# Raw self-attention scores copied to SBUF and masked there, in a two-layer transformer kernel on one Trainium2 core

## What is computed

```python
# layer 0
Q, K, V = relu(x @ Wq.T + bq), relu(ctx @ Wk.T + bk), relu(ctx @ Wv.T + bv)
scores = einsum('bqd,bkd->bqk', Q_, K_) / sqrt(d)
scores = where(key_mask == 0, NEG, scores); scores = where(tril == 0, NEG, scores)
attn = softmax(scores) * query_mask
x = gamma * norm(attn @ V_ + x) + beta
# layer 1
q, k, v = heads(split(layernorm(x) @ sa_wqkv))
wei = softmax(where(padding, -inf, where(causal, q @ k.T * scale, -inf)))
result = x + merge(wei @ v) @ sa_wproj + sa_bproj
q2 = heads(layernorm(result) @ ed_wq); k2, v2 = heads(split(layernorm(ctx) @ ed_wkv))
result = result + merge(softmax(q2 @ k2.T * scale) @ v2) @ ed_wproj + ed_bproj
result = result + relu(layernorm(x) @ ff_w1 + ff_b1) @ ff_w2 + ff_b2
```

## Time and profile before

| | us |
|---|---|
| median of three runs | 370.42 |
| the profiled execution, its own time | 373.18 |
| its span in the profile | 371.3 |
| TensorE busy with matmuls | 353.6 (95%) |
| VectorE busy | 224.9 (61%) |
| ScalarE busy | 172.1 (46%) |
| GpSimd busy | 52.6 (14%) |

### The profile page before, as it was taken

The page is one execution under the profiler, slowest core; times in us unless marked ns, Lnnn a source line. Parts: engine busy times, 40 slices in busy tenths (PEclk is TensorE's granted clock), DMA queues, the critical chain, the costliest instruction groups (busy, mean ns, idle before and its releaser), DMA issues.

```text
span 371.3 us, 9714 instructions
## 1 busy us (share of the span) xinstructions
PE 353.6 (95%) x4154; PEld 267.0 (72%) x4154; DVE 224.9 (61%) x563; ACT 172.1 (46%) x301; POOL 52.6 (14%) x67
## 2 busy tenths in 40 slices
PE   8997899999999999999999998999999999999995
PEld 4575778987886857875678676765986758785673
DVE  3289998915658677646686646478954374354511
ACT  2336755273682341565515155593353455505142
POOL 2003351122240100012210012132110121000000
PEclk9789999999999999999999999999999999999999
DMA  6757012100000012000000001000000000000000
GB/s 188 209 215 302 26 26 72 39 2 2 2 25 2 3 26 85 2 14 0 17 1 3 2 15 71 2 14 14 3 0 4 2 2 12 3 2 14 2 2 25
DMA packets 5044, 13.43 MB, mean 36 GB/s; under 512 B 669, under 2 KB 2837, under 8 KB 4746
## 3 DMA queue, kind: packets, MB, share of 16 engines
q1 hardware_dynamic: 4712, 12.72, 10.4%
q10 hardware_dynamic: 290, 0.10, 0.1%
HBM read 11.89 MB, written 0.92 MB: 35 GB/s over the span
## 4 chain that ended last, share of the span: by engine, by line
PE 81%; DVE 11%; ACT 5%; issue 2%; POOL 0%; DVEq 0%
PE ring L503 39%; PE ring L757 8%; PE acc L661 7%; PE ring L636 5%; PE ring L771 5%; PE ring L616 4%; DVE negmax L1053 4%; ACT exps L877 3%; PE ring L610 3%; PE ring L648 2%; PE ring L680 2%; DVE negmax L1032 1%; PE ring L815 1%; PE ring L628 1%; PE ring L722 1%
## 5 line engine op out<-in xcount | busy, mean ns | idle before, releaser
L1053 DVE TENSOR_REDUCE negmax<-ring 112x2 f32<-112x750 f32 x64 | 56.9, 935 | 32.9 <-PE ring L757 32.8
L877 ACT ACTIVATE exps<-ring 125x896 f32<-125x896 f32 x48 | 41.4, 915 | 56.7 <-PE ring L771 56.6
L1264 POOL TENSOR_SCALAR_AFFINE_SELECT exps<-exps 112x896 f32<-112x896 f32 x32 | 31.3, 1000 | 111.5 <-ACT exps L877 111.5
L1032 DVE TENSOR_REDUCE negmax<-ring 112x8 f32<-112x896 f32 x32 | 33.4, 1086 | 19.4 <-PE ring L616 19.3
L661 PE MATMUL acc<-exps,v 125*17 125x112 f32 (+1 forms) x1280 | 38.7, 261 | 0.3 <-ACT exps L877 0.2
L757 PE MATMUL ring<-k,q 32*112 32x376 f32 x256 | 37.7, 518 | 1.3 <-ACT exps L877 0.7
L661 PEld LDWEIGHTS acc<-exps,v 125*17 125x17 f32 (+1 forms) x1280 | 28.1, 97 | 13.9 <-issue 9.5
L877 ACT ACTIVATE exps<-ring,pad 112x896 f32<-112x896 f32 x32 | 30.5, 1004 | 15.5 <-PE ring L648 15.4
L503 PE MATMUL ring<-w_b,h 128*112 128x256 f32 x128 | 29.4, 383 | 0.0
L503 PEld LDWEIGHTS ring<-w_b,h 128*112 128x112 f32 x128 | 22.0, 177 | 6.1 <-DVE negmax L1053 0.6
L914 ACT ACTIVATE h<-ring,flat_c 128x224 f32<-128x224 f32 x32 | 11.7, 448 | 31.7 <-PE ring L503 31.7
(11 more groups left out here) (149 smaller groups left out, 551.5 us busy)
## 6 DMA issues: line engine op xcount, KB each, us to landing
c_nat<-in_ctx SPq DMA_DIRECT2D x4, 750.0 KB
w_b<-in_w_b SPq DMA_DIRECT2D x1, 2304.0 KB, 9.9
xk_t<-in_xk_t SPq DMA_DIRECT2D x8, 224.0 KB, 4.3
w_a<-in_w_a SPq DMA_DIRECT2D x1, 1280.0 KB, 5.6
xh<-in_keys SPq DMA_DIRECT2D x4, 224.0 KB, 3.8
x_nat<-in_x SPq DMA_DIRECT2D x4, 224.0 KB, 3.3
out<-x SPq DMA_DIRECT2D x8, 112.0 KB, 1.8
w_qk<-in_w_qk SPq DMA_DIRECT2D x2, 256.0 KB, 4.3
```

Source lines behind the costliest of these rows:

```text
L877: return nc.scalar.activation(exps[0:k, EXP_AT[job], :, :], o[0:k, :, 0:4 * T], ACT.Exp, bias=bias)
L1032: v_max[b].step(nc.vector.tensor_reduce(negmax[0][:, slot(g, b), 2 * m_:2 * m_ + 2, :], o[0:T, :, 0:4 * T].rearrange("p r (j t) -> p r j t ...
L1053: x_max[b].step(nc.vector.tensor_reduce(negmax[1][:, b, 2 * m_:2 * m_ + 2, i], o[0:T, :, 0:S], AX.X, ALU.max, negate=True), g, 2 * i + m_ + 1)
L1264: p_masked[b].step(nc.gpsimd.affine_select(e, e, [[0, 8], [1, T]], ALU.is_ge, 0.0, base=0, channel_multiplier=-1), g, k)
```

## The change

Step `S` no longer writes the mask in PSUM: its first product in each bank starts the bank. ScalarE copies the raw scores of each pair of banks to one of two new SBUF tiles, `low` (112 x 2 x 8 x 112, float32); GpSimd adds the mask there in place (`scores_masked`); and a new step `Z` places VectorE's maxima, which read `low` in place of PSUM. The bank is now given back by ScalarE's copy. A tile of `low` is written again only when the maxima of the step two before it are taken.

The additive mask is now needed with queries on partitions. Step `masks` turns the four tiles with four more products (112x112, bf16), and VectorE copies them to `mask_q`. The steps `rows` on TensorE and ScalarE are gone: two transfers on SyncE's queue write the vectors to all partitions at once, 125 KB after `w_v0` and 560 KB between `w_a` and `w_b`; one VectorE addition sums the last two vectors. `MIX` is a new string, with the 16 letters of the `Z` steps in it.

```diff
 def c_steps(g, b):
-    return [("S", g, 0, b), ("M", g, 0, b), ("X", g, 0, b), ("V", g, 0, b), ("O", g, 0, b), ("dev", g, b), ("norm", g, b),
-            ("S", g, 1, b), ("M", g, 1, b), ("X", g, 1, b), ("V", g, 1, b), ("O", g, 1, b)]
+    return [("S", g, 0, b), ("Z", g, 0, b), ("M", g, 0, b), ("X", g, 0, b), ("V", g, 0, b), ("O", g, 0, b), ("dev", g, b), ("norm", g, b),
+            ("S", g, 1, b), ("Z", g, 1, b), ("M", g, 1, b), ("X", g, 1, b), ("V", g, 1, b), ("O", g, 1, b)]
...
-MIX = ("RARLALNNDNECAECDNCPJWCNCWDPIEWJICPDDCJPIDNDJPJAIPAAJAIDIHCHDCPJIEPCEEDCIDJCDHAHJPIPAJAKAINAPAEBIBJNBIJABEPBENBPBBBEFBFEB"
+MIX = ("ALALNNDNEEDNCANJDCPWWIWDCPJECDJIINDPDICCJDPCIPCIPAJAAIAJCDHJHCCPDCDEDJCIPDCDERAPEAAJKJANIAAHAJIIFIPABEPJIBNJBIJCFEBEDPBF"
...
 masks (TensorE)
-                end(nc.tensor.matmul(o[0:T, 0, G:2 * G], tril[:, :], keep0b[:, slot(g, 0):slot(g, G)], start=False, stop=True, skip_group_check=True))
+                nc.tensor.matmul(o[0:T, 0, G:2 * G], tril[:, :], keep0b[:, slot(g, 0):slot(g, G)], start=False, stop=True, skip_group_check=True)
+                for i in range(2 * G):
+                    m = nc.tensor.matmul(o[0:T, 0, 8 + i * T:8 + (i + 1) * T], add_mask[:, i // G, slot(g, i % G), :], ident_b[:, :], start=False, stop=True, skip_group_check=True)
+                end(m)
...
 self_scores (TensorE)
-                if l == 0:
-                    pe.wait_ge(*v_mask.at(g, 7 + 2 * b))
...
-                for r in range(R):
-                    nc.tensor.matmul(bank(r)[0:T, 0:4 * T], add_mask[:, l, slot(g, b), :], ident_b[:, :].unsqueeze(1).to_broadcast([T, 4, T]),
-                                     start=True, stop=False, skip_group_check=True)
...
-                                                 kf[g % 2][32 * r:32 * r + 32, c, b, :], start=False, stop=True, skip_group_check=True)
+                                                 kf[g % 2][32 * r:32 * r + 32, c, b, :], start=j == 0, stop=True, skip_group_check=True)
...
 ScalarE
+            def scores_copied(g, l, b):
+                if ("S", g, l, b) in SCORES_BEFORE:
+                    _, g_old, l_old, b_old = SCORES_BEFORE["S", g, l, b]
+                    act.wait_ge(*v_max[b_old].at(g_old, 2 * l_old + 2))
+                for m_ in range(2):
+                    o = is_filled(act, ("S", g, l, b, m_))
+                    a_exp[b].step(nc.scalar.activation(low[LOW_AT["S", g, l, b]][:, m_, :, :].rearrange("p (r j) t -> p r (j t)", r=2), o[0:T, :, 0:4 * T], ACT.Copy), g, 4 * l + m_ + 1)
...
 VectorE, now at step Z
             def self_maxima(g, l, b):
                 for m_ in range(2):
-                    o = is_filled(dve, ("S", g, l, b, m_))
+                    dve.wait_ge(*p_masked[b].at(g, 4 * l + m_ + 1))
...
 GpSimd
+            def scores_masked(g, l, b):
+                pool.wait_ge(*v_cnt.done(g))
+                for m_ in range(2):
+                    part = low[LOW_AT["S", g, l, b]][:, m_, :, :]
+                    pool.wait_ge(*a_exp[b].at(g, 4 * l + m_ + 1))
+                    p_masked[b].step(nc.gpsimd.tensor_tensor(part, part, mask_q[:, l, slot(g, b), :].unsqueeze(1).to_broadcast([T, 8, T]), ALU.add), g, 4 * l + m_ + 1)
...
 SyncE
+            sp.dma_start(rows_sb[:, 0:U], row_d[:, 0:U].to_broadcast([CH, U])).then_inc(bv_loaded, 16)
...
                 sp.dma_start(w_a[:, :], w_d["a"]).then_inc(wa_loaded, 16)
+                sp.dma_start(rows_sb[0:T, U:6 * U], row_d[:, U:6 * U].to_broadcast([T, 5 * U])).then_inc(rows_loaded, 16)
                 sp.wait_ge(kv_loaded, 16)
```

More of the change, by code:

```diff
@@ L141, in jobs_of @@
         return [("counts", step[1])]
-    if kind == "rows":
-        return [("rows", 0, step[1])]
     return [step] if kind in ("shift", "q0", "k0", "v0", "M", "O", "xT", "q1", "k1", "v1", "t1", "proj", "xqT", "q2", "h", "cT", "k2", "v2", "cM", "cO", "t2", "f", "y") else []
@@ L205 @@
 SUMS_BEFORE = dict(zip(SUMS[1:], SUMS))
+SCORES = [step for step in ORDER if step[0] == "S"]
+LOW_AT = {step: i % 2 for i, step in enumerate(SCORES)}
+SCORES_BEFORE = dict(zip(SCORES[2:], SCORES))
+for new_, old_ in SCORES_BEFORE.items():
+    assert PLACE[("Z",) + old_[1:]] < PLACE[new_], (old_, new_)
 def build(nc, xk_t_d, x_nat_d, keys_d, c_nat_d, c_t_d, c_first_d, mask_d, w_d, flat_d, mask_const_d, row_d, out_d):
@@ L282, in build @@
         add_mask = sb("add_mask", [T, 2, 2 * G, T], BF16)
+        mask_q = sb("mask_q", [T, 2, 2 * G, T], BF16)
+        low = [sb(f"low{i}", [T, 2, 8, T]) for i in range(2)]
         v_all_g = sb("v_all_g", [T, B, U])
@@ L1236, in _ @@
             dve.wait_ge(prep_dve, PREP_DVE)
-            run({"flag": flag, "general": general, "f": add_hidden, "split": weights_lo, "keys": keys, "masks": masks, "late": late_masks, "v0": values0, "S": self_maxima, "M": self_spread, "O": self_out, "dev": deviation0, "norm": norm1,
+            run({"rows": rows_summed, "flag": flag, "general": general, "f": add_hidden, "split": weights_lo, "keys": keys, "masks": masks, "late": late_masks, "v0": values0, "Z": self_maxima, "M": self_spread, "O": self_out, "dev": deviation0, "norm": norm1,
                  "v1": values1, "proj": residual1, "norm2": norm2,
```

85 lines of the change are left out of this document (35 added, 50 removed).

## The result

The changed kernel takes 392.32 us (median of four runs, 388.29 to 393.98) where the kernel before takes 371.68 beside it: a ratio of 1.057, 95% interval 1.050 to 1.064. 357.6 was forecast, in a range of 349.5 to 365. The profiled execution took 390.83, its span is 389.1.

What follows compares the result with a forecast made beforehand. After 40 us TensorE's issued products were taken to bound the kernel. Mask products -14.4, rows -2.0, turning products +1.6 and a start wait +2.0 gave -12.8 us: median 370.42 to 357.6, range 349.5 to 365.

Steps and rivals of the forecast that it cites:

- What goes: On TensorE: the mask products leave, 14.4 us, and the `rows` products, 3.65 us, of which 2.0 counted as gain.
- A product taken away is time taken away: TensorE after 40 us: each removed product shortens the kernel by its own time, unless its operands come later than before.
- the chain's own part: Scores to maxima: 3.0 us becomes about 7.1, covered about as tightly as before; no wait booked in the full stretch.
- The rows products: TensorE's bias-row products at the start: 3.65 us in all, of which 2.0 us was counted as coming back.
- The start: First 40 us: eight additions precede the first select on GpSimd; 2.0 us of TensorE wait ahead of the first `V`.
- So the mask moves up as well: At the start: the flag comes 2.5 us earlier, so VectorE's key sums and the mask behind it come earlier.
- The lock: Rival: GpSimd's additions collide with VectorE, costing it 16 us, +12 on the kernel, 369.6; chance 0.05 for nothing left.
- VectorE loses nothing and gains nothing: VectorE's maxima: the same 896 elements at 1.09 us each, with no gain from reading SBUF.
- The clock: TensorE's low clock between 14 and 22 us may stretch or move with gaps; 2.0 of 2.51 us counted for that.
- More than forecast: Rival: TensorE's gaps from 40 to 360 us and its clock at the start may shrink, -8 us, 349.6; chance 0.13.
- the rival on the other side: GpSimd: a slow addition of 3.9 us gives +30, 388; slower than before from about 2.9; chance 0.05.
- All four signs of being wrong: Idle time ahead of L621, L1026 waiting on `low`, L1100 at a mean well over 0.5 us, low clock beyond 22 us.

Runs made afterwards that it cites:

- o_no_mask: The kernel before without its 64 mask products, in its own order, the mask left out of the maxima; 363.38 us beside 369.18.
- o_dummy_adds: The kernel before with 32 extra GpSimd additions of the changed kernel's shape, on a tile nobody else touches; 390.97 us, ratio 1.061.
- n_no_add: The changed kernel with GpSimd's 32 mask additions each replaced by a memset of one column, mask left out of the maxima; 376.05 us, ratio 1.016.
- n_keys_early: The changed kernel with group 1's keys loaded before the context of group 0, nothing else changed; 385.98 us, ratio 1.045.

## Why the prediction was wrong

357.6 was forecast and 392.3 measured, 34.7 us apart. By medians, whose kernel before differs by up to 3 us from one set of runs to another, 23 of them go with the additions and the late keys. Of the other 11.8, 5.8 lie between the forecast and the 363.4 of o_no_mask, which only takes the mask products out, and 6.0 between that and the 369.4 without additions and with early keys: the copies, handovers, turned masks and the order, which no run sizes one by one. Three steps of the prediction failed.

**The term "What goes"** was nearly right as work and wrong as time. TensorE's work fell by 14.2 us; 14.4 + 3.65 - 1.6 = 16.4 had been counted (the page's busy time, which was to fall by 13 to 15, fell by 2.8, since it has the low clock in it). "A product taken away is time taken away" failed: o_no_mask gave back 7 of 13.6. About 4 of the rest turned into waits, so those were products under which the other engines did what TensorE needs next. The windows of the earlier trace rows show 97% busy; they do not show how little lies between a result and its use, and the "2.9 to 3.4 for a chain of 3.0" in the chain's own part did.

**The rows products** were sized right: 2.0 forecast, about 2 measured in executions at full clock. What became of them inside the changed kernel is not seen apart from the next point.

**The start.** "So the mask moves up as well" looked at the first group. For the second I read in the order that its `masks` step now stands ahead of `S`, and put its products into the lead of that `S`, but did not ask when its keys land. They are issued at 11.77 us behind `c_nat` and land at 23.9. I booked 2.0 us of wait; TensorE idled 6.88 in one piece, and the first `V`, forecast at 35 to 37 us, began at 43.66. Early keys alone bring back 4 to 6 us.

**The lock** is the largest error: "VectorE loses nothing and gains nothing" looked at its maxima alone, and the sum has no term for what the additions do to its other operations. As a rival it had 16 us of lost VectorE time; 20.6 were measured (23.1 less the mask copies). Of that it let 12 reach the kernel; the additions alone cost 22.3 in o_dummy_adds, with the low clock that came with the waits. So VectorE's loss was sized well, its way to TensorE at about half, and its weight was not good: a chance of 0.05. Two arguments misled me. "VectorE is idle for 39%": the operations it holds up are those on which TensorE is about to wait. "8 us or more of products stand over each such chain": three operations in a row lost 4.2 us at 75 us (5.49 for 1.26), and the maxima queue behind them. I also named only operations with two inputs; half of the casualties have one, among them the casts in the spread maxima themselves.

**The clock** was in the sum as a remark. It cost 11.4 us more than in the profile of before, the second loss after the idle time. Each gap of 3.9 us or more between 19 and 26 us came with a low stretch that began in it or within 2 us behind it: 20 us at 0.50 in after, 17 in n_no_add, 14 in o_dummy_adds and n_keys_early. Score products of 1.05 us take 1.85 in it.

**"More than forecast"** and the reverse sign: the rival on the other side needed an addition of 2.9 us. It came at 1.91, and the kernel was slower all the same, by 20 us. The bound on that side rested on one mechanism, the length of the addition, and left the lock out.

Of what I said would show: additions of 1.8 to 2.1, `S` of 1.0 us and ScalarE at 200 (197.8) came true. All four signs of being wrong showed: idle time ahead of L621 (7.3 us), L1026 waiting on `low` (7.1 us), L1100 at a mean of 0.70, and a low clock beyond 22 us.

## What to carry to other kernels

Before work goes to an idle GpSimd, list what VectorE does on SBUF meanwhile, two inputs or one (reductions and one-element operations were spared here): each such operation can last until the GpSimd instruction ends, and if it leads to the next product, price that as time of TensorE. A dummy copy of the new work, dropped into the old kernel, measures this in one run. Time taken from a full TensorE is worth only as much as the chains under it can shorten; here it was half (7 of 13.6 us), and a run without the products tells. For every step that moves forward look up when its load is issued.
